# A two-layer cross-attention and expert kernel: the first batch's chunk statistics, second query copy and next batch's row statistics in other places of the engines' orders

## The reference, cut to what matters

```
x = x + gated_attention(layernorm(x), ctx)      # L0: layernorm of x and of ctx with gamma, beta; rope; temporal bias; gate
x = x + tanh(layernorm(x) @ W @ A1 @ A2 + b)
x = x + attention(layernorm(x), ctx)            # L1: raw ctx, no rope, no bias (mask of ones)
x = x + top2_of_8_experts(layernorm(x))
# inside L0, for the context:
kv = (ctx - mean) * rsqrt(var + eps) * gamma + beta ;  k = rope(kv @ Wk.T) ;  v = kv @ Wv.T
probs = softmax(q @ k.T / sqrt(8) + bias) ;  out = probs @ v
```

## Time and profile before

| | |
|---|---|
| runs | 596.02, 596.11, 601.25 us |
| profiled execution | span 599.1 us; its own time is not printed beside it; of the three runs only that of 601.25 us can hold this span |
| PE busy | 520.1 us, 87% of the span |
| ACT busy | 430.9 us, 72%; of it 398.3 in 416 exponentials |
| DVE busy | 280.5 us, 47% |
| POOL busy | 168.2 us, 28% |
| mean granted PE clock | 0.956 |
| DMA | 74.5 MB, mean 124 GB/s |

### The profile page before, as it was taken

How to read it: one execution, slowest core, us unless ns; L and a number is a source line. 1 busy time by engine, 2 the same in 40 slices (tenths; PEclk the granted TensorE clock), 3 DMA queues, 4 the chain that set the end, 5 groups by cost and what they waited for, 6 DMA issues and landing times.

```text
span 599.1 us, 15308 instructions
## 1 busy us (share of the span) xinstructions
PE 520.1 (87%) x6318; PEld 261.9 (44%) x6318; DVE 280.5 (47%) x718; ACT 430.9 (72%) x492; POOL 168.2 (28%) x199
## 2 busy tenths in 40 slices
PE   7678799878888998899999999999999999999960
PEld 4344454434444554455554445434443444344330
DVE  5636655863586435564431342235352534434064
ACT  1327487662767887787879997898989879997901
POOL 5355836485268233780101001000001000000000
PEclk9869999996899999999999999999999999999976
DMA  8396955449544823475184374129214902000000
GB/s 274 83 273 177 282 199 126 140 161 316 149 144 130 289 86 78 133 217 171 26 166 134 85 173 116 30 71 201 71 39 129 211 6 57 7 2 10 2 1 13
DMA packets 51581, 74.50 MB, mean 124 GB/s; under 512 B 11146, under 2 KB 40050, under 8 KB 51506
## 3 DMA queue, kind: packets, MB, share of 16 engines
q1 hardware_dynamic: 41554, 38.32, 25.6%
q0 software_dynamic: 5632, 24.07, 12.2%
q10 hardware_dynamic: 4320, 11.09, 6.1%
HBM read 39.95 MB, written 18.83 MB: 98 GB/s over the span
## 4 chain that ended last, share of the span: by engine, by line
PE 52%; ACT 15%; DVE 13%; issue 9%; POOL 5%; DMA 2%; SPq 2%; ACTq 0%; DVEq 0%
PE ps L496 20%; ACT probs L1089 13%; PE ps L474 13%; PE ps L409 3%; DVE k_swapped L1374 2%; PE ps L582 2%; PE ps L399 2%; DVE row_stats L1336 1%; PE ps L508 1%; PE ps L403 1%; DMA q_side<-in_far_q 1%; DVE k_parts L1391 1%; DMA wvg_columns<-in_wvg_columns 1%; DVE inverse L1462 1%; SPq L777 1%
## 5 line engine op out<-in xcount | busy, mean ns | idle before, releaser
L1089 ACT ACTIVATE probs<-ps 124x1024 f32<-124x1024 f32 (+1 forms) x416 | 398.3, 1024 | 94.0 <-PE ps L479 66.2
L496 PE MATMUL ps<-probs,values 124*9 124x256 f32 (+1 forms) x3328 | 222.2, 385 | 3.1 <-DVE out_sums L1458 2.9
L474 PE MATMUL ps<-q_side,k_side 64*124 64x256 bf16 (+1 forms) x1664 | 164.6, 294 | 32.1 <-ACT probs L1089 29.6
L474 PEld LDWEIGHTS ps<-q_side,k_side 64*124 64x124 bf16 (+1 forms) x1664 | 80.6, 132 | 137.1 <-ACT probs L1089 100.1
L496 PEld LDWEIGHTS ps<-probs,values 124*9 124x9 f32 (+1 forms) x3328 | 71.2, 90 | 91.3 <-issue 32.9
L985 POOL TENSOR_TENSOR post_rstd<-post_rstd,power 128x2 f32<-128x2 f32 x12 | 8.5, 705 | 154.3 <-DVE post_rstd L1565 94.7
L931 POOL DMA_DIRECT2D mask_q<-in_mask x16 | 8.9, 559 | 130.7 <-DVE checks L1433 111.6
L479 PE MATMUL ps<-bias_near,bias_w 64*124 64x84 bf16 (+1 forms) x416 | 42.9, 202 | 0.0
L1374 DVE SCALAR_TENSOR_TENSOR k_swapped<-ps,beta_products,k_table_sb 32x496 f32<-32x496 f32 (+2 forms) x64 | 40.4, 632 | 0.9
L1443 DVE TENSOR_REDUCE sample_max<-ps 128x8 f32<-128x512 f32 x32 | 20.5, 686 | 33.9 <-PE ps L432 33.8
L409 PE MATMUL ps<-w_centred,ctx_turned 128*124 128x256 f32 (+1 forms) x104 | 30.7, 418 | 3.5 <-DVE k_swapped L1374 1.7
(11 more groups left out here) (213 smaller groups left out, 523.4 us busy)
## 6 DMA issues: line engine op xcount, KB each, us to landing
k_side<-k_scratch SPq DMA_DIRECT2D x24, 400.2 KB, 8.6
k_side<-k_parts SPq DMA_DIRECT2D x48, 124.0 KB, 2.4
k_scratch<-k_parts POOLq DMA_DIRECT2D x16, 372.0 KB, 5.5
q_side<-q_parts SPq DMA_DIRECT2D x69, 64.0 KB, 2.5
v_scratch<-values POOLq DMA_DIRECT2D x4, 936.0 KB, 9.6
values<-v_scratch SPq DMA_DIRECT2D x4, 936.0 KB, 15.2
v_scratch<-v POOLq DMA_DIRECT2D x12, 288.0 KB, 5.2
mask_q<-in_mask POOLq DMA_DIRECT2D x8, 400.5 KB, 3.5
```

The costliest lines, as they stand in the source:

```text
L474: last = pe.matmul(ps[0:width, bank, SQ * i:SQ * (i + 1)], kst[rows, j % 2, 2 * g + i, at], qst[rows, query_slot(j, run), 2 * g + i, :], s ...
L496: last = pe.matmul(ps[32 * i:32 * i + VC, ACC + g // 2, SQ * (g % 2):SQ * (g % 2) + SQ], v[0:rows, j % 2, t, h, :], p[0:rows, u % 4, SQ * ...
L1089: act.activation(p[0:rows, u % 4, :], ps[0:rows, s:s + 2, :].rearrange("p a n -> p (a n)"), ACT.Exp)\
```

## The change

On DVE, the statistics of chunk 2 move ahead of `rotate_keys(0, 1)`, its norm and chunk 3's statistics between the values of chunk 0 and those of chunk 1, and chunk 3's norm behind chunk 1's values. Chunks 2 and 3 each get a `power_of` of their own, the first behind POOL's low parts of chunk 0, the second inside `second_parts(1)`. PE spreads chunk 2 into ACC behind `keys(0, 0, 1)`, and chunk 3 into ACC+1 behind `scores(1)`; the two clearings go, since four earlier multiplications of zeros now take ACC and ACC+1 too; `values(0)` and `values(2)` wait until the spreads are read. The second query copy moves from SP to ACT's queue, in two groups of three DMAs. For batch 1, `row_deviations(1)` stands ahead of `keys(0, 3)` on DVE, `power_of_rows(1)` ahead of `parts(0, 3)` on POOL, the store and loads ahead of `place_keys(0, 3)` on SP, and the load of its token rows moves from step 5 to step 2. The `x` statistics of the other batches move to between the rotation and the values of chunk 2.

```diff
--- before.py
+++ after.py
@@ -484,6 +484,8 @@
             def values(u):
                 j, t, g = u // UB, u % UB // NG, u % NG
                 rows = rows_of(t)
+                if u in (0, 2):
+                    pe.wait_ge(cn_ready, 3 + u // 2)
                 pe.wait_ge(probs_ready, u + 1)
                 if j < NB and g == 0 and t in [t0 for t0, _ in CHUNKS]:
                     bank, n = last_values([t0 for t0, _ in CHUNKS].index(t))
@@ -654,7 +656,7 @@
                               start=True, stop=True, skip_group_check=True)
 
             pe.wait_ge(zeroed, 1)
-            keep_busy(10)
+            keep_busy(10, (0, 1, ACC, ACC + 1))
             centre_weights()
             keep_busy(3)
             pe.wait_ge(ident_in, 16)
@@ -673,7 +675,9 @@
                 sample(0, c)
             keys(0, 0, 1)
 
-            keep_busy(6, (4,))
+            pe.wait_ge(rs_ready, 3)
+            spread_rstd(ACC, 2).then_inc(r_spread, 1)
+            keep_busy(5, (ACC + 1,))
             turn_maxima(0)
             for k in (1, 2):
                 keys(0, 1, k)
@@ -681,15 +685,8 @@
             for u in range(2):
                 scores(u)
 
-            pe.wait_ge(rs_ready, 3)
-            for n in (2, 3):
-                pe.wait_ge(cn_ready, n - 1)
-                spread_rstd(n + 2, n).then_inc(r_spread, 1)
-            pe.wait_ge(cn_ready, 4)
-            for n in range(2):
-
-                pe.matmul(ps[:, ACC + n, :], zeros[:], zeros[:].unsqueeze(1).broadcast_to((128, 4, 128)),
-                          start=True, stop=True, skip_group_check=True)
+            pe.wait_ge(rs_ready, 4)
+            spread_rstd(ACC + 1, 3).then_inc(r_spread, 1)
             for u in range(0, NJ * UB, 2):
                 j, pair = u // UB, u % UB // 2
                 for w in (u + 2, u + 3):
@@ -721,7 +718,7 @@
                 sp.dma_start(ct[:, k_0:k_1], G["ctx_t"][0, :, k_0:k_1]).then_inc(ct_in[n], 16)
 
             def store_rstd(b):
-                sp.wait_ge(rs_ready, b + 3)
+                sp.wait_ge(rs_ready, b + NC)
                 sp.dma_start(G["r_dram"][b].rearrange("(p t) -> p t", t=KT), rs_row[:]).then_inc(r_out, 16)
 
             def load_rstd(b):
@@ -846,16 +843,15 @@
             load_shift(0)
             place_keys(0, 1)
             place_far(0, 1)
-            place_queries(0, 1, q2_in)
             place_shift(0, 1, shift2_in)
-            sp.dma_start(G["pick"][:], G["pick_in"]).then_inc(pick_in, 16)
             place_far(0, 2)
             place_keys(0, 2)
+            store_rstd(1)
             place_far(0, 3)
-            place_keys(0, 3)
-            store_rstd(1)
             load_rstd_tiles(1)
             load_rstd(1)
+            place_keys(0, 3)
+            sp.dma_start(G["pick"][:], G["pick_in"]).then_inc(pick_in, 16)
             place_far(0, 4)
             load_queries_of(1)
             place_far(1, 0)
@@ -938,11 +934,11 @@
 
             def power_of(t0, t1):
 
-                pool.wait_ge(var_done, 1 if t0 == 0 else 2 if t1 < KT else 3)
+                pool.wait_ge(var_done, 1 + CHUNKS.index((t0, t1)))
                 pool.tensor_tensor(rs[0:TS, 0, t0:t1], rs[0:TS, 0, t0:t1], power[0:TS, t0:t1], ALU.pow).then_inc(rs_ready, 1)
 
             def power_of_rows(b):
-                pool.wait_ge(var_done, b + 3)
+                pool.wait_ge(var_done, b + NC)
                 pool.tensor_tensor(rs_row[:], rs_row[:], power[:, 0:KT], ALU.pow).then_inc(rs_ready, 1)
 
             def x_power(n, t0, t1):
@@ -1017,6 +1013,8 @@
                 w = CHUNK_KEYS[n][1] - CHUNK_KEYS[n][0]
                 pool.wait_ge(seen[HIGH], side.of(HIGH, "k1", 0, n))
                 pool.tensor_tensor(k1[:, n, 0:w], k1[:, n, 0:w], kp1[:, n, 0, 0:w], ALU.subtract).then_inc(rest1, 1)
+                if n == 1:
+                    power_of(*CHUNKS[3])
                 pool.wait_ge(mid1, n + 1)
                 pool.tensor_tensor(kp1[:, n, 2, 0:w], k1[:, n, 0:w], kp1[:, n, 1, 0:w], ALU.subtract).then_inc(lo1, 1)
 
@@ -1029,20 +1027,20 @@
             high_parts(0)
             power_of(*CHUNKS[1])
             low_parts(0)
+            power_of(*CHUNKS[2])
             second_parts(0)
             high_parts(1)
             low_parts(1)
             second_parts(1)
-            power_of(CHUNKS[2][0], KT)
             for n in range(2):
                 store_keys(0, n)
             ones_of_values(1)
             parts(0, 2)
             store_keys(0, 2)
             x_power(1, 2, XT)
+            power_of_rows(1)
             parts(0, 3)
             store_keys(0, 3)
-            power_of_rows(1)
             for b in range(1, NB):
                 for n in range(NC):
                     norm_context(b, n)
@@ -1141,6 +1139,13 @@
                 act.wait_ge(q_rest, k + 1)
                 act.activation(qp[:, 1, cols], q[:, cols], ACT.Copy).then_inc(q_mid, 1)
 
+            def place_second_queries(which):
+
+                for r in which:
+                    part = TERMS[r][0]
+                    act.wait_ge((q_hi, q_mid, q_lo)[part], 1)
+                    act.dma_start(qst[r::HD, query_slot(0, 1), :, :], qp[:, part, columns(0)]).then_inc(q2_in, 16)
+
             def load_table(n):
                 k_0, k_1 = CHUNK_KEYS[n]
                 act.dma_start(k_table[:, 2 * k_0:2 * k_1], G["k_table"][:, 2 * k_0:2 * k_1]).then_inc(table_in[n], 16)
@@ -1166,7 +1171,7 @@
                     place_far_keys(act, 0, 2)
                     act.dma_start(G["bias_w"][:, TS * 5:SKP], G["bias_k"][:, TS * 5:SKP]).then_inc(bias_in[2], 16)
                     act.dma_start(near[:, 5:KT, :], G["near_q"][:, 5:KT, :]).then_inc(bias_in[2], 16)
-                elif (j, i) == (0, 5):
+                elif (j, i) == (0, 2):
                     load_token_rows(1)
                 elif (j, i) == (0, 16):
                     load_turned(1)
@@ -1201,8 +1206,10 @@
             middle_queries(0)
             place_first_queries(act, 0, (1, 2))
             second_keys(0, 0)
+            place_second_queries((0, 1, 4))
             second_keys(0, 1)
             middle_of_second(0, 0)
+            place_second_queries((2, 3, 5))
             high_of_first(1)
             middle_of_first(1)
             middle_of_second(0, 1)
@@ -1708,22 +1715,27 @@
             rest_of_queries(0)
             norm_context(1)
             low_queries(0)
+            token_stats(2)
+            deviations(*CHUNKS[2])
             rotate_keys(0, 1)
             for c in range(2):
                 sample_maxima(0, c)
             make_shift(0)
             both_values(0, 0, 0)
+            norm_context(2)
+            token_stats(3)
+            deviations(*CHUNKS[3])
             for k in range(2):
                 both_values(0, 1, k)
-            for n in (2, 3):
-                token_stats(n)
-            deviations(CHUNKS[2][0], KT)
-            for n in (2, 3):
-                norm_context(n)
-            keys(0, 2)
+            norm_context(3)
+            rotate_keys(0, 2)
             x_deviations(2, XT)
+            both_values(0, 2, 0)
+            high_part(0, 2)
+            both_values(0, 2, 1)
+            middle_part(0, 2)
+            row_deviations(1)
             keys(0, 3)
-            row_deviations(1)
             for k in range(2):
                 norm_queries(k)
                 turn_queries(k)
```

## The result

Twenty executions of the changed kernel took 588.01 to 603.77 us, median 598.12; twenty of the kernel before took 594.22 to 604.28, median 597.54. The ratio is 0.9898, with a 95% interval of 0.9849 to 0.9946. The ratio leaves out executions over 1.5% above the fastest of the same kernel, and since the changed kernel's fastest is at 588.0, it rests on four of its twenty executions (588.0, 588.2, 594.5, 594.6); the other sixteen lie at 596.9 to 603.8. The medians stand at 1.001. The change lowered the best time by 6 us and left the usual one where it was. What follows says why both are true.

The account below looks back on a forecast made before the run. PE and ACT feed each other over the span; the change touches only two early PE holes. Gains of 7.3 and 2.4 us sum to 9.7, so 596.1 - 9.7 = 586.4 us, range 582.5 to 592.5.

Parts of the forecast that it names:

- within 1%: Whole kernel: outcome where the time can't be told from no change, within 5.96 us; chance 0.16.
- The median as the base: Sum: subtract the 9.7 us gain from the median 596.1, not from the profiled execution of 601.25 us.
- first hole: PE before scores(2): chunks 2 and 3's statistics delay it; scores(2) moves from 40.67 to 33.5 us, 7.3 us carried.
- What I costed at nothing: DVE's moved statistics, POOL's two powers and six DMA issues on ACT: free or 0 to 0.1 us each.
- The keys of chunk 1: Before scores(4): last DMAs issued by 31.85 us take 4.7 us, land by 36.5 us; gain there 7.2 us.
- Rival C: Before scores(4): chunk 1's keys land late, POOL's earlier stores meeting them; 588.8 us, or 590.4; chance 0.13.
- Second hole: PE's wait for the query norm before slot 15 (L373): 3.62 us falls to 1.2, gain 2.4 us.
- some 1.7 us: DVE in chunk 3: high part, two value pieces and middle part between POOL's steps and the query norm.
- the rest of the program keeps its distances: Behind both holes: later work moves along, with no further gain or loss.
- E: Behind 90 us: the gain is absorbed by a load or wait that does not move; 590.2 to 602 us; chance 0.09.
- F: Batch 0: PE's clock falls, values cost 0.85 us more per pair; 607 us in all; chance 0.06.
- clock 0.50 past 45 us: PE: the sign that would show the clock falling in batch 0, with its price of 20 us.

Follow-up runs that it names:

- again: The changed kernel unedited, run and profiled a second time; median 597.86 us, ratio 0.994 to the kernel before.
- first_only: The changed kernel with batch 1's row statistics, power, store and loads, token rows and x statistics placed as before; median 597.39 us, ratio 0.9953.
- second_only: The kernel before with only batch 1's row statistics, power, store and loads and the x statistics moved as in the change; median 596.18 us, ratio 0.9993.
- copy_on_sp: The changed kernel with the second query copy back on SP's queue behind chunk 1's keys; median 597.86 us, ratio 1.0018.
- stores_late: The changed kernel with POOL's stores of chunks 0 and 1 held until chunk 1's keys have landed; median 598.19 us, ratio 1.0003.
- x_late: The changed kernel with ACT's two x loads at step 4 instead of step 1; median 596.95 us, ratio 0.9969.
- all_late: bulk_late with chunk 3's key table loaded at step 8 and ACT's wait for the shift rows removed; median 592.20 us, ratio 0.987.
- bulk_late: The changed kernel with x loads at step 4, token rows at step 6, far keys and bias at step 7; median 591.80 us, ratio 0.9888.
- after: The changed kernel's first profiled execution, against the kernel before; 588.17 us, span 585.9 us.
- bulk_late_2: The kernel of bulk_late unchanged, run and profiled once more; median 593.89 us, ratio 0.9918.

## Why the prediction was right and wrong

**In number.** 586.4 us was not met. The three executions at 588 are nearest; the median, 598.12, is above the range. Only the ratio came out on the forecast's side: 0.9898 of 596.1 is 590.0 us, inside the range. That is luck, since it rests on four executions and two of them are the good ones near 588; the forecast was made for the usual execution. By the medians the outcome is "within 1%", to which I had given 0.16.

**The median as the base.** The profiled execution before lay 5.1 us above the median, "and no view says where"; I took the difference from the median. The table suggests where: the profile has the remainder of 528.1 us, lost mostly at the turn, behind both holes. If a usual execution before has the other one, it takes 71 + 522.4 + 2.15 = 595.6 us, which is where the lower group of the kernel before lies. No profile of such an execution was taken, so this is argued, not shown; by it the step was right.

**Statistics, spreads, clearings (first hole).** Right, in every profile: scores(2) at 31.1 to 32.6 us where I had 33.5. The spreads ran at full clock (1.15 us). What I costed at nothing (DVE's statistics, POOL's two powers, the copy on ACT) put none of it off.

**The keys of chunk 1: the step that failed.** I took 4.7 us from the earlier trace rows and wrote "so they land by 36.5 us". It is a duration from an execution in which ACT's loads came behind those DMAs (`x` at 31.66 us). The first profile after had them there too (31.61), took 4.8 us and met the forecast, 36.58 for 36.5; that was luck. In the five profiles with the `x` load at 29.8 to 30.1 us (again, first_only, second_only, copy_on_sp, stores_late) it is 7.2 to 10.4 us. The place of that load would have told of it: it stands behind the first exponential, whose time shifts with PE's clock, while SP's keys do not. Rival C had the place ("scores(4) waits for k_side"), with a price of 2.4 to 4 us and the wrong source, POOL's stores. The measured price is 41.42 - 36.5 = 4.9 us, plus half clock behind it, and the source is ACT's loads: stores_late leaves it (40.75), x_late takes it away (35.99), all_late takes the rest (33.81). The rule that I had weighed there (the Trainium skill, DMA: Bandwidth & Descriptors, Queues, rings and completion order: round robin over the busy rows) would, by the prediction's estimate for a third queue, give 2.4 us of delay; the rows give 2.5 to 5.7 (7.2 to 10.4 instead of 4.7). The Trainium skill says on the same page (Issuing engines are not separate DMA queues) that all issuers share the 16 DMA engines and interleave; with that the rows agree, 2.4 us with ACT's loads and the table away, 4.0 to 4.8 with the table or loads behind the keys, up to 10.4 with the loads of `x` ahead of the last of them.

**Second hole.** The mechanism is right: the wait before L373 is 0.78 us (1.2 forecast), DVE waits 2.51 us for POOL, the power of 13 columns is late next, and second_only gives 1.6 to 2.75 us against 2.4. But a term of its chain was too small. In the first profile scores(4) is on time, and L373 still starts at 63.56 instead of 61.3. About 1.0 us of this was lost by batch 1's statistics (49.22 instead of 48.2), which waited for chunk 2's values. The rest is DVE's work from chunk 3's sum to the query norm, "some 1.7 us" in the prediction: it took 62.78 - 59.93 = 2.85 us. The profile before has the same piece, from this row to the statistics at 66.51, and there too it is 2.86 us:

```profile
63.65 0.42 DVE L1385 CAST k_parts<-k 128x485 bf16<-128x485 f32 x1 [0.86 <-POOL k L959]
```

**What follows: "the rest of the program keeps its distances".** This failed too, and it is the other half of the lost gain. The distance behind L373 has two levels, some 4 to 6 us apart, by the clock at the turn. If the two groups of the kernel before are these levels, it has the lower one in 79 of 101 executions. With the table the changed kernel's groups read so (2.15 us lie around the span): keys in time and the turn at full clock, 63.56 + 522.3 + 2.15 = 588.0, is the group at 588, three executions; keys late and full clock, 68.89 + 522.4 + 2.15 = 593.4, is nearest to the one at 594.5, six (keys in time and half clock, 63.56 + 527.4 + 2.15 = 593.1, can't be told from it by the time); keys late and half clock, 68.89 + 527.4 + 2.15 = 598.4, is the group at 597 to 604, 23. That reading of executions without a profile goes by their times and mean clocks (0.969 to 0.975, 0.961 to 0.965, 0.946 to 0.963) and is argued, not shown; the last group is 7 us wide, more than the distance between the levels. By it the change gains 2 us at L373 in a usual execution and loses 5.6 us at the turn in three of four. Why the half clock comes more often once PE is early (6 of 12 in second_only too), no run settles. It is what rivals E and F had in part, E the place behind 90 us, F the clock; F's price of 20 us was far off, and its sign, clock 0.50 past 45 us, came in again only at the turn.

**Sum by what was measured.** With full clock at the turn the profiles can be set side by side: second_only 590.7 us, bulk_late 588.1, after 585.9, their L373 at 68.27, 64.87 and 63.56. From second_only, the first hole gives 4.7 us in after and 3.4 in bulk_late, of the 7.3 forecast, although scores(4) in bulk_late is 42.60 - 35.27 = 7.3 us earlier. The other half goes where bulk_late has waits that second_only lacks: ACT's 1.79 us for a store and DVE's 3.25 for `x`. DVE's 2.50 us for POOL stands in both. No run takes these waits away one by one, so how the loss divides among them is not shown. Both holes together are worth 3.4 + 2.75 = 6.2 us at L373 with the keys in time, not 9.7; beside bulk_late_2, whose first scores (30.27) came as late as those of before (30.76), it is 71.02 - 64.44 = 6.6. The version with the loads in order has medians of 591.80 and 593.89 against 596.89 and 596.55 of the kernel before beside it, 5.1 and 2.7 us less, and is the best of all here with all_late (592.20).

## What to carry to other kernels

When a long wait is removed, list the transfers that were issued in its shadow and ask for each whether it is ordered behind the next consumer's DMA by a dependency or only by time; here 1.6 MB of loads that nobody needed yet took the place of the removed hole. Giving them a later place took the median from 597.9 to 598.1 down to 591.8 to 593.9 us. A landing time read from one execution of full DMA engines is no price: look at what is issued just before and behind it, and bound it by a second execution. And split a span at the end of the changed stretch: start of the unchanged part and remainder showed two effects that the medians hid in each other.

## What the runs showed of the hardware

One DMA of 124 KB took 2.4, 4.0, 4.8, 7.2 and 10.4 us to land in the same place of the program, by what ACT had issued around it. The DMA share over 30 to 36 us was 0.98 to 1.09 where it took 4.8 (after) and 10.4 (again), and 0.74 to 0.81 where it took 2.4 (all_late). Two executions of one program, which differ first in PE's clock before 33 us (scores(0) at 30.34 or 28.99), ended 10.3 us apart, 588.17 and 598.47: the one that was later at 30 us ended first, 5.3 us ahead at L373 and 5.1 more behind it. From L373 to the second L391 the same work of the same kernel took 74.8 us with a granted clock of 1.00 at its end and 78.7 with 0.50 (bulk_late and its repeat). The clock fell behind a PE wait of 2.88 us in all fourteen profiles, and was back at 1.00 within 10 us, to stay there, in four of them. A power of 13 columns on POOL took 2.70 us and of four 1.02, and the issue of the six DMAs of the query copy 3.56 us on ACT against 3.89 on SP.
